# Graph attention and a top-2 expert layer on one core: two of four column groups of P in full precision

## The chip, the cores and the metric

The kernel runs on one core of a Trainium2 chip. A core has five engines with queues of their own: PE (TensorE, matrix products), DVE (VectorE), ACT (ScalarE), POOL (GpSimd) and SP (SyncE, here only DMA issues). They run side by side and wait for one another by semaphores. The metric is device time in microseconds (us) of one execution; less is better.

## The reference

```python
def gnn(x, adj, W, a):                       # x is layer-normalised, 4096 x 256
    Wh = x @ W
    e = leaky_relu((Wh @ a[:256])[:, None] + (Wh @ a[256:])[None, :], 0.2)
    e = where((adj > 0) | eye, e, -9e15)     # 4096 x 4096
    return softmax(e, axis=1) @ Wh
x = x + gnn(layernorm(x), adj, W, a)
# then a mixture of 8 experts: router, softmax, the best 2, and for each
# token the weighted sum of W2 @ gelu(W1 @ xe + b1) + b2 of its 2 experts
x = x + ffn(layernorm(x), Wr, br, ln_g, ln_b, W1, b1, W2, b2)
```

The inputs and outputs are float32, and the adjacency matrix has 4096 x 4096 entries.

## The kernel before, in words

Each engine has its own program, written out by hand; the order inside a program is the order in the code, and semaphores tie the programs together. There are three stages.

**Projection** (to about 69 us). x comes in as 32 tiles of 128 rows, is normalised, transposed and multiplied by W. Each tile of Wh stays in SBUF as the right operand of the attention product. Tiles 0 to 23 are kept as two float16 tensors, a high part (`wh[:, n, 0]`, written by ACT in L872) and a rest (`wh[:, n, 1]`, by DVE in L1070). Tiles 24 to 31 are kept in float32 in `wh32`.

**Attention** (about 69 to 690 us). A step i handles 128 rows of the 4096 x 4096 scores. DVE computes the scores of two steps ahead in two halves (`scores`, L1099) and masks those of the next step and takes their minimum (`masked`, L1107); ACT turns the adjacency rows into a bias (L854) and takes the exponentials (L884). The result P, 128 x 4096, is needed transposed. PE transposes it in G = 4 column groups of 8 blocks (`p_transpose`, L707) through two PSUM buffers `tp`; ACT copies a group out, scaled (`p_hi`, L892). Of groups 0 to GS - 1 that copy is float16, `pt_hi`, and DVE computes the rest of the rounding as a second float16 tensor (`p_lo`, L1112, into `pt_lo`). PE then multiplies (`av`): for a float16 group three products a block, high by high, high by rest and rest by high (L723 to L725), 24 in all; for a float32 group one product a block (L727), 8 in all. GS was 3: groups 0, 1 and 2 are float16 and group 3 is float32.

In the same loop earlier rows go on their way: step i - 1 is divided by its sum and added to x (L1118, L1122, L1130), its statistics are taken (L1136, L1143), POOL computes the scales (`row_scales`, L534 to L543) and DVE normalises it (`normalise1`, L1152). Step i - 2 has its router logits computed (PE L741, DVE L1160, L1166, L1171), its top two kept (`keep_top`, L1174 and L1179), turned into one-hots (L1183, L1184, L1188), and its position in the lists of the experts counted by PE (`router_pos`, L746 and L747). Step i - 3 gets its destination rows (`positions` to `keep_rows`, L1192 to L1203), and POOL scatters it to DRAM (L567). POOL also splits the weights of the experts into two float16 parts, one chunk a step (`split_w`, L525 and L528), and clears the diagonal of the mask (`diagonal`, L505).

The order of PE in a step is transposes 0 and 1, av of group 3 of the step before, the router's transposes (L733), av 0, logits (L741), transpose 2, av 1, transpose 3, av 2, router_pos. That of POOL is `cast_w` (L516), gates (L550 to L559), scatter (L567 twice), split_w, diagonal, row_scales. The code of DVE for a step has these lines in the part that the change touches:

```python
                if router:
                    experts(i - 2)
                if now:
                    p_lo(i, 2)
                if router:
                    keep_top(i - 2, u)
                if within(i, 0, T - 3):
                    scores(i + 2, u, 0)
```

**Experts** (about 690 us to the end). The scattered rows come back expert by expert, and PE multiplies them by the two float16 parts of W1 and W2 (L804 to L806, L820, L823). The change touches nothing of this stage.

Of the kernel before, what the change touches and what calls it, by code (L numbers as in the profile page):

```python
# [7 lines left out]
F32 = mybir.dt.float32  # L8
# [5 lines left out]
P = 128  # L14
# [8 lines left out]
def build(nc, x, adj, gnn_w, gnn_a, w_r, b_r, ln_g, ln_b, w1, b1, w2, b2, out):  # L23
# [16 lines left out]
    N, D = x.shape  # L40
    E = w_r.shape[1]
    HID = w1.shape[2]
    T = N // P
    KD = D // P
    HC = HID // P
    G = 4
    GJ = T // G
    GW = GJ * P
# [5 lines left out]
    RING = 4  # L54
    CHUNKS = 4
    CW = KD * HID // 2
    GS = G - 1
    TS = GS * GJ
    XC = 8
    TC = T // XC  # L60
# [15 lines left out]
    with ExitStack() as ctx:  # L76
        def sb(name, shape, dt, stack=ctx):
            return stack.enter_context(nc.sbuf_tensor(name, shape, dt))

        def sem(name):  # L80
            return ctx.enter_context(nc.semaphore(name))
# [25 lines left out]
        front = ExitStack()  # L107
# [3 lines left out]
        t2_row = sb("t2_row", [P, N], F32, front)  # L111
        sc = [sb(f"sc{u}", [P, N], F32, front) for u in range(2)]
        wh = sb("wh", [P, TS, 2, D], F16, front)
        wh32 = sb("wh32", [P, GJ, D], F32, front)
        pt_hi = [sb(f"pt_hi{g}", [P, GW], F16, front) for g in range(GS)]
        pt_lo = [sb(f"pt_lo{g}", [P, GW], F16, front) for g in range(GS)]
        pt32 = sb("pt32", [P, GW], F32, front)
        x_late = sb("x_late", [P, N], F32, front)
        wsp = [sb(f"wsp{u}", [P, 2 * CW], F16, front) for u in range(2)]
        xn = [sb(f"xn{u}", [P, D], F32, front) for u in range(2)]  # L120
# [112 lines left out]
        s_hi = sem("p_hi_done")  # L233
        s_lo = sem("p_lo_done")
# [87 lines left out]
        def within(i, first, last):  # L322

            return not isinstance(i, int) or first <= i <= last
# [142 lines left out]
        def _(pool):  # L467
# [50 lines left out]
            def split_w(e, q):  # L518

                i = CHUNKS * e + q  # L520
                u = q % 2
                pool.wait_ge(s_lo, GS * i + 2)
                pool.wait_ge(s_wf[u], 16 * (2 * e + q // 2 + 1))
# [132 lines left out]
        def _(pe):  # L656
# [41 lines left out]
            def p_transpose(i, u, g):  # L698
                if g % 2 == 0:
                    pe.wait_ge(s_e[g // 2], i + 1)  # L700
                if g == 1:
                    if within(i, 1, T):
                        pe.wait_ge(s_hi, G * i)
                elif g > 1 or within(i, 1, T):
                    pe.wait_ge(s_lo, GS * i + max(g - 1, 0))
                for c in range(GJ):
                    m = pe.transpose(tp[g % 2][:, c * P:(c + 1) * P], sc[u][:, (GJ * g + c) * P:(GJ * g + c + 1) * P], ident[:, :])  # L707
                m.then_inc(s_t, 1)

            def av(i, u, g):  # L710

                o = acc[u][:, 0:D]
                if g < GS:
                    pe.wait_ge(s_lo, GS * i + g + 1)
                else:
                    pe.wait_ge(s_hi, G * i + G)
                if g == 0 and within(i, 2, T):
                    pe.wait_ge(s_x1, X1 * (i - 2) + 3)
                for c in range(GJ):
                    j = GJ * g + c  # L720
                    cols = slice(c * P, (c + 1) * P)
                    if g < GS:
                        pe.matmul(o, pt_hi[g][:, cols], wh[:, j, 0, :], start=(j == 0), stop=False)  # L723
                        pe.matmul(o, pt_hi[g][:, cols], wh[:, j, 1, :], start=False, stop=False)  # L724
                        m = pe.matmul(o, pt_lo[g][:, cols], wh[:, j, 0, :], start=False, stop=False)  # L725
                    else:
                        m = pe.matmul(o, pt32[:, cols], wh32[:, c, :], start=False, stop=(c == GJ - 1))  # L727
                m.then_inc(s_av, 1)

            def router_t(i, r):  # L730
# [116 lines left out]
        def _(act):  # L847
# [39 lines left out]
            def p_hi(i, g):  # L887
                act.wait_ge(s_t, G * i + g + 1)
                if within(i, 1, T):
                    act.wait_ge(s_av, G * i + g - 3)  # L890
                dst = pt_hi[g] if g < GS else pt32
                act.activation(dst[:, :], tp[g % 2][:, :], ACT.Copy, scale=PSCALE).then_inc(s_hi, 1)  # L892

            def gate_exp(n, u):
# [108 lines left out]
        def _(dve):  # L1003
# [106 lines left out]
            def p_lo(i, g):  # L1110
                dve.wait_ge(s_hi, G * i + g + 1)
                dve.scalar_tensor_tensor(out=pt_lo[g][:, :], in0=tp[g % 2][:, :], scalar=PSCALE, in1=pt_hi[g][:, :],  # L1112
                                         op0=ALU.mult, op1=ALU.subtract).then_inc(s_lo, 1)


            def row_sum(n, u):
                dve.wait_ge(s_e[1], n + 1)
                dve.tensor_scalar(rinv[:, 0:1], rsum[u][:, 0:1], rsum[u][:, 1:2], PSCALE, ALU.add, ALU.mult).then_inc(s_x1, 1)  # L1118

            def row_reciprocal(n):  # L1120
                dve.wait_ge(s_x1, X1 * n + 1)
                dve.reciprocal(rinv[:, 1:2], rinv[:, 0:1]).then_inc(s_x1, 1)  # L1122
# [67 lines left out]
            def positions(n):  # L1190
                dve.wait_ge(s_pos, n + 1)
                dve.tensor_tensor(posb[:, :], rt_ps[:, 16:16 + E], count[:, :], ALU.add).then_inc(s_next, 1)  # L1192
# [13 lines left out]
            def attend(i, r, o):  # L1206

                u = r % 2
                v = 1 - u
                now, ahead = within(i, 0, T - 1), within(i, 0, T - 2)  # L1210
                behind, router, ranks = within(i, 1, T), within(i, 2, T + 1), within(i, 3, T + 2)
                back = (r + RING - 1) % RING
                back_o = o if r > 0 else o - 1
                if ranks:
                    positions(i - 3)
                if behind:
                    row_sum(i - 1, v)
                if ranks:
                    choose_rows(i - 3)
                if behind:  # L1220
                    row_reciprocal(i - 1)
                if ranks:
                    keep_rows(i - 3, (r + 1) % RING)
                if now:
                    p_lo(i, 0)
                    p_lo(i, 1)
                if ahead:
                    masked(i + 1, v)
                if behind:
                    add_attention(i - 1, v, back, back_o)  # L1230
                if router:
                    logits(i - 2, u)
                if behind:
                    stats1(i - 1, back)
                if router:
                    largest(i - 2)
                if behind:
                    moments1(i - 1)
                if router:
                    experts(i - 2)  # L1240
                if now:
                    p_lo(i, 2)
                if router:
                    keep_top(i - 2, u)
                if within(i, 0, T - 3):
                    scores(i + 2, u, 0)
                if router:
                    one_hots(i - 2, u)
                if behind:
                    normalise1(i - 1, v, back, back_o)  # L1250
                if router:
                    both_hots(i - 2)
                if within(i, 0, T - 3):
                    scores(i + 2, u, 1)
# [6 lines left out]
            for i in range(2 * RING):  # L1261
                attend(i, i % RING, i // RING)
# [151 lines left out]
```

## Time and profile before

| what | value |
|---|---|
| median of 3 runs | 1116.82 us (1110.28 to 1117.27) |
| the profiled execution | 1116.05 us, span of the trace 1114.5 us |
| PE busy | 983.5 us, 88% |
| DVE busy | 822.2 us, 74% |
| POOL busy | 814.8 us, 73% |
| ACT busy | 579.3 us, 52% |
| mean granted TensorE clock | 0.957 of full speed |

The span goes from the first to the last instruction; the profiled execution took 1.55 us more than that. The shares are of the span and mix three stages with different limits. A mean duration of a group counts each instruction from its own start to its own end, and neighbouring matrix products overlap, so that the distance between two starts can be much smaller than the duration.

### The profile page before, as it was taken

What the parts mean: (1) busy time and instruction counts of PE and PEld (TensorE: products, weight loads), DVE (VectorE), ACT (ScalarE), POOL (GpSimd) and SP (SyncE); (2) the same over time, 40 slices, a digit from 0 to 9 for tenths busy, and PEclk for the clock granted to TensorE, in tenths of its full rate; (3) what the DMA queues carried; (4) which work ended last, traced back from release to release, by engine and by line L of the source; (5) the groups of instructions that cost most, each with busy time, mean ns of one, the idle gap of its engine ahead of it and who ended that gap; (6) DMA issues with size and microseconds to landing.
All of it is one profiled execution on the core that took longest, in us unless ns stands there. A gap on an engine that the chain in (4) does not pass through costs nothing. (4 is left out here: it accounts for less than half of the span.)

```text
span 1114.5 us, 25515 instructions
## 1 busy us (share of the span) xinstructions
PE 983.5 (88%) x7566; PEld 822.3 (74%) x7567; DVE 822.2 (74%) x1563; ACT 579.3 (52%) x906; POOL 814.8 (73%) x910
## 2 busy tenths in 40 slices
PE   5959988899898888898988992799999999999995
PEld 4847877788787778787877882677777777777763
DVE  6859878888888888888887865457676666757663
ACT  3667676666675766676665740343433333343341
POOL 2218777888797888797878864278888888878763
PEclk9979999999999999999999996899999999999998
DMA  8164748575658485667566627774233232322231
GB/s 246 14 210 156 270 153 264 183 248 174 229 176 269 155 264 168 228 187 252 172 220 205 195 92 254 241 235 119 44 52 51 44 57 39 56 43 49 39 45 19
DMA packets 92201, 170.46 MB, mean 153 GB/s; under 512 B 19952, under 2 KB 69360, under 8 KB 83824
## 3 DMA queue, kind: packets, MB, share of 16 engines
q1 hardware_dynamic: 57296, 133.00, 34.5%
q0 software_dynamic: 24048, 26.23, 14.3%
q10 hardware_dynamic: 10800, 10.52, 3.1%
q8 instruction: 30, 0.49, 0.2%
q14 instruction: 27, 0.22, 0.1%
HBM read 136.91 MB, written 41.19 MB: 160 GB/s over the span
## 5 line engine op out<-in xcount | busy, mean ns | idle before, releaser
L723 PE MATMUL acc<-wh,pt_hi 128*128 128x256 f16 x768 | 211.2, 275 | 2.8 <-DVE pt_lo L1112 2.8
L971 ACT ACTIVATE hf<-tp,b_cols 128x256 f32<-128x256 f32 (+1 forms) x312 | 116.1, 459 | 187.4 <-PE tp L806 183.3
L724 PE MATMUL acc<-wh,pt_hi 128*128 128x256 f16 x768 | 211.2, 275 | 0.0
L725 PE MATMUL acc<-wh,pt_lo 128*128 128x256 f16 x768 | 211.1, 275 | 0.0
L567 POOL DMA_INDIRECT rows_dram<-rows,slot x64 | 161.3, 2520 | 38.6 <-POOL rows L559 26.4
L639 POOL DMA_INDIRECT out<-y_sb,yidx x71 | 118.9, 1674 | 92.2 <-issue 42.8
L820 PE MATMUL acc<-w_sb,h_hi 128*128 x568 | 170.9, 379 | 5.1 <-issue 3.8
L892 ACT ACTIVATE pt_hi<-tp 128x1024 f16<-128x1024 f32 x96 | 96.2, 1022 | 144.8 <-PE tp L707 144.4
L804 PE MATMUL tp<-x_hi,w_sb 128*128 128x256 f16 (+1 forms) x624 | 162.2, 265 | 2.6 <-DVE x_lo L1345 2.5
L806 PE MATMUL tp<-x_down,w_sb 128*128 128x256 f16 (+1 forms) x624 | 162.3, 265 | 0.0
L805 PE MATMUL tp<-x_lo,w_sb 128*128 128x256 f16 (+1 forms) x624 | 161.9, 265 | 0.0
L707 PE MATMUL tp<-ident,sc 128*128 128x128 f32 x1024 | 143.8, 294 | 14.2 <-ACT sc L884 12.4
L1099 DVE SCALAR_TENSOR_TENSOR sc<-t_row,s_col 128x2048 f32<-128x2048 f32 x64 | 151.6, 2372 | 0.1
L854 ACT ACTIVATE bias_sb<-adj_sb,big 128x2048 bf16<-128x2048 f32 x64 | 127.5, 2001 | 42.0 <-DMA adj_sb<-in_adj 41.7
L614 POOL TENSOR_SCALAR dz<-xs,dump 128x1 f32<-128x1 f32 x71 | 143.5, 2716 | 5.0 <-DMA xs<-rows_dram 3.9
L1107 DVE CUSTOM_DVE_ANT_0 sc<-sc,bias_sb 128x4096 f32<-128x4096 f32 x32 | 141.3, 4416 | 0.2 <-DVE sc L1099 0.2
L707 PEld LDWEIGHTS tp<-ident,sc 128*128 128x128 f32 x1024 | 126.4, 153 | 16.5 <-issue 14.7
L1112 DVE SCALAR_TENSOR_TENSOR pt_lo<-tp,pt_hi 128x1024 f16<-128x1024 f32 x96 | 115.5, 1221 | 25.6 <-ACT pt_hi L892 25.1
L884 ACT ACTIVATE sc<-sc,mn 128x2048 f32<-128x2048 f32 x64 | 127.6, 1994 | 2.8 <-DVE mn L1107 2.8
L1342 DVE CAST x_hi<-xg 128x512 f16<-128x512 f32 (+1 forms) x39 | 22.8, 584 | 138.9 <-ACT xg L960 127.1
L727 PE MATMUL acc<-wh,pt 128*128 128x256 f32 x512 | 122.7, 395 | 0.0
L823 PE MATMUL acc<-w_sb,h_lo 128*128 x568 | 113.0, 273 | 0.0
(170 smaller groups left out, 1953.9 us busy)
## 6 DMA issues: line engine op xcount, KB each, us to landing
adj_sb<-in_adj SPq DMA_DIRECT2D x64, 1024.0 KB
x_late<-in_L_ffn_W SPq DMA_DIRECT2D x32, 512.0 KB
wsplit_dram<-wsp SPq DMA_DIRECT2D x32, 512.0 KB, 2.9
w_sb<-wsplit_dram SPq DMA_DIRECT2D x32, 512.0 KB, 5.6
xs<-rows_dram ACTq DMA_DIRECT2D x32, 260.0 KB, 3.5
wsp<-in_L_ffn_W POOLq DMA_DIRECT2D x32, 256.0 KB
x<-in_x SPq DMA_DIRECT2D x32, 128.0 KB, 2.5
out<-x SPq DMA_DIRECT2D x32, 128.0 KB, 2.3
```

What stands on the lines that cost most here:

```text
L567: pool.indirect_dma_start(out=rows_dram[:, :], out_offset=bass.IndirectOffsetOnAxis(ap=slot[r][:, k:k + 1], axis=0), in_=rows[r][:, :], in ...
L614: pool.tensor_scalar(dz[:, s:s + 1], xs[r][:, s, D + 3:D + 4], 0.0, dump[:, s:s + 1], ALU.is_equal, ALU.mult).then_inc(s_dz, 1)
L707: m = pe.transpose(tp[g % 2][:, c * P:(c + 1) * P], sc[u][:, (GJ * g + c) * P:(GJ * g + c + 1) * P], ident[:, :])
L723: pe.matmul(o, pt_hi[g][:, cols], wh[:, j, 0, :], start=(j == 0), stop=False)
L724: pe.matmul(o, pt_hi[g][:, cols], wh[:, j, 1, :], start=False, stop=False)
L725: m = pe.matmul(o, pt_lo[g][:, cols], wh[:, j, 0, :], start=False, stop=False)
L804: pe.matmul(o, w_hi, x_hi[:, cols], start=(k == 0), stop=False)
L805: pe.matmul(o, w_hi, x_lo[:, cols], start=False, stop=False)
L806: m = pe.matmul(o, w_lo, x_down[:, cols], start=False, stop=(k == KD - 1))
L820: pe.matmul(acc[s][:, :], h_hi[u][:, (c * ns + s) * P:(c * ns + s + 1) * P], w_both, start=(c == 0), stop=False, skip_group_check=True)
L1099: dve.scalar_tensor_tensor(out=sc[u][:, cols], in0=t_row[:, cols], scalar=s_col8[:, bass.ds(n, 1)], in1=t2_row[:, cols], op0=ALU.add, op1= ...
L1107: dve.tensor_tensor_reduce(sc[u][:, :], sc[u][:, :], bias_sb[u][:, :], 1.0, 3.0e38, ALU.add, ALU.min, mn[u][:, 0:1]).then_inc(s_b, 1)
```

## The change

GS becomes G // 2 = 2, so that groups 0 and 1 of P stay float16 pairs and groups 2 and 3 are float32. Tiles 16 to 23 of Wh move from the float16 pair to `wh32`, and `pt32` becomes two buffers. Group 2 needs no `p_lo`, and DVE's call in the middle of the step goes. The waits in front of the transposes follow: a transpose that overwrites a `tp` buffer waits for whichever reads it last, ACT's copy where the group is float32 and DVE's `p_lo` where it is float16.

```diff
-    GS = G - 1
+    GS = G // 2
@@
-        wh32 = sb("wh32", [P, GJ, D], F32, front)
+        wh32 = sb("wh32", [P, T - TS, D], F32, front)
@@
-        pt32 = sb("pt32", [P, GW], F32, front)
+        pt32 = [sb(f"pt32{g}", [P, GW], F32, front) for g in range(GS, G)]
@@ p_transpose
-                if g == 1:
-                    if within(i, 1, T):
-                        pe.wait_ge(s_hi, G * i)
-                elif g > 1 or within(i, 1, T):
-                    pe.wait_ge(s_lo, GS * i + max(g - 1, 0))
+                if g >= GS:
+                    pe.wait_ge(s_lo, GS * i + g - GS + 1)
+                elif within(i, 1, T):
+                    pe.wait_ge(s_hi, G * (i - 1) + GS + g + 1)
@@ av
-                    pe.wait_ge(s_hi, G * i + G)
+                    pe.wait_ge(s_hi, G * i + g + 1)
@@
-                        m = pe.matmul(o, pt32[:, cols], wh32[:, c, :], start=False, stop=(c == GJ - 1))
+                        m = pe.matmul(o, pt32[g - GS][:, cols], wh32[:, j - TS, :], start=False, stop=(j == T - 1))
@@ p_hi
-                dst = pt_hi[g] if g < GS else pt32
+                dst = pt_hi[g] if g < GS else pt32[g - GS]
@@ attend of DVE
-                if now:
-                    p_lo(i, 2)
```

On PE the end of a step of the attention loop (the last block of av 2, router_pos, and the first transposes of the next step) reads so before:

```order
L723 MATMUL acc<-wh,pt_hi 128x256
L724 MATMUL acc<-wh,pt_hi 128x256
L725 MATMUL acc<-wh,pt_lo 128x256
L746 MATMUL rt_ps<-oh,tri 128x8 [waits onehot_done]
L747 MATMUL rt_ps<-oh,ones 128x8
L337 REGISTER_ALU
L337 COMPARE_AND_BRANCH
L707 MATMUL tp<-ident,sc 128x128 [waits p_lo_done,exp_half_done0]
L707 MATMUL tp<-ident,sc 128x128 x7
L707 MATMUL tp<-ident,sc 128x128 [waits p_hi_done]
```

and the same place of the changed kernel, from transpose 3 on (its lines are numbered one lower from here on):

```order
L706 MATMUL tp<-ident,sc 128x128 [waits p_lo_done]
L706 MATMUL tp<-ident,sc 128x128 x7
L715 ISA
L726 MATMUL acc<-wh,pt 128x256 [waits p_hi_done]
L726 MATMUL acc<-wh,pt 128x256 x7
L745 MATMUL rt_ps<-oh,tri 128x8 [waits onehot_done]
L746 MATMUL rt_ps<-oh,ones 128x8
L337 REGISTER_ALU
L337 COMPARE_AND_BRANCH
L706 MATMUL tp<-ident,sc 128x128 [waits p_hi_done,exp_half_done0]
```

The 24 float16 products of av 2 became 8 float32 products, which wait for ACT's copy alone, and the first transpose of the next step waits for that copy in place of `p_lo`.

On DVE the middle of a step, from the statistics of step i - 1 to its normalisation, reads so before:

```order
L1143 BN_AGGR mv<-bs 128x2 [waits x1_step,ln_var_eps_step]
L1171 MAX_INDEX idx<-top,lg 128x8 [waits router_step]
L1112 SCALAR_TENSOR_TENSOR pt_lo<-tp,pt_hi 128x1024 [waits p_hi_done]
L1174 TENSOR_TENSOR gap_l<-top 128x1
L1179 CAST idxf<-idx 128x2 [waits row_tags_done,router_step]
L1099 SCALAR_TENSOR_TENSOR sc<-t_row,s_col 128x2048 [waits p_transposed]
L1183 TENSOR_SCALAR oh<-iota_e,idxf 128x8 [waits router_step]
L1184 TENSOR_SCALAR oh<-iota_e,idxf 128x8
L1152 TENSOR_SCALAR rows<-x_0,mv,rs 128x256 [waits rows_scattered0,ln1_rstd,ln1_stats]
```

and in the changed kernel:

```order
L1142 BN_AGGR mv<-bs 128x2 [waits x1_step,ln_var_eps_step]
L1170 MAX_INDEX idx<-top,lg 128x8 [waits router_step]
L1173 TENSOR_TENSOR gap_l<-top 128x1
L1178 CAST idxf<-idx 128x2 [waits row_tags_done,router_step]
L1098 SCALAR_TENSOR_TENSOR sc<-t_row,s_col 128x2048 [waits p_transposed]
L1182 TENSOR_SCALAR oh<-iota_e,idxf 128x8 [waits router_step]
L1183 TENSOR_SCALAR oh<-iota_e,idxf 128x8
L1151 TENSOR_SCALAR rows<-x_0,mv,rs 128x256 [waits rows_scattered0,ln1_rstd,ln1_stats]
```

The rounding rest of group 2 and its wait for ACT are gone, and everything behind it follows directly on the router's index search.

## Rows read from the trace of the kernel before

**Rows 1.** Waits from 70 to 640 us: waiter, releaser, total us, times, longest.

```profile
PE rt_ps L746 <- DVE oh L1188: 43.6, 24, 2.7
DVE rows L1152 <- POOL rs L540: 40.6, 25, 2.1
```

**Rows 2.** Timeline of PE, the step from 411 us: start, duration, what, idle before.

```profile
411.37 0.18 PE L746 MATMUL rt_ps<-oh,tri 128*128 128x8 bf16 x1 [1.36 <-DVE oh L1188]
...
413.36 3.62 PE L727 MATMUL acc<-wh,pt 128*128 128x256 f32 x16
416.82 0.38 PE L733 MATMUL xt_ps<-ident,rows 128*128 128x128 f32 x2
...
424.42 0.27 PE L723 MATMUL acc<-wh,pt_hi 128*128 128x256 f16 x1
424.53 0.27 PE L724 MATMUL acc<-wh,pt_hi 128*128 128x256 f16 x1
...
429.81 0.18 PE L746 MATMUL rt_ps<-oh,tri 128*128 128x8 bf16 x1 [2.61 <-DVE oh L1188]
```

**Rows 3.** Timeline of DVE in the same step.

```profile
416.44 4.42 DVE L1107 CUSTOM_DVE_ANT_0 sc<-sc,bias_sb 128x4096 f32<-128x4096 f32 x1
...
422.30 1.21 DVE L1112 SCALAR_TENSOR_TENSOR pt_lo<-tp,pt_hi 128x1024 f16<-128x1024 f32 x1
423.43 0.46 DVE L1174 TENSOR_TENSOR gap_l<-top 128x1 f32<-128x1 f32 x1
...
423.89 2.34 DVE L1099 SCALAR_TENSOR_TENSOR sc<-t_row,s_col 128x2048 f32<-128x2048 f32 x1
...
429.27 0.41 DVE L1152 TENSOR_SCALAR rows<-x,mv,rs 128x256 f32<-128x256 f32 x1 [1.99 <-POOL rs L540]
```

**Rows 4.** Timeline of POOL in the same step.

```profile
417.26 4.43 POOL L567 DMA_INDIRECT rows_dram<-rows,slot  x1 [0.30 <-issue]
421.71 2.15 POOL L525 TENSOR_TENSOR x_late<-x_late,wsp 128x1024 f32<-128x1024 f32 x1
424.07 3.06 POOL L528 TENSOR_SCALAR wsp<-x_late 128x1024 f16<-128x1024 f32 x1 [0.21 <-POOL x_late L525]
427.21 0.43 POOL L505 TENSOR_TENSOR bias_sb<-bias_sb,off_diag 128x128 bf16 x1
```

**Rows 5.** Single lines of the whole trace: durations in ns, least, median and most.

```profile
L525 POOL TENSOR_TENSOR x_late<-x_late,wsp x32: 2129/2141/6247, 86.4 to 659.4; 128x1024 f32<-128x1024 f32 x32
L528 POOL TENSOR_SCALAR wsp<-x_late x32: 1039/1040/3072, 92.9 to 661.7; 128x1024 f16<-128x1024 f32 x32
```

**Rows 6.** Windows of PE after three router_pos: length, PE busy, granted clock, DMA.

```profile
392.25:397.90 5.65, 5.65 (x28) 0.70 0.96 335
411.37:416.40 5.03, 5.03 (x33) 1.00 0.99 390
429.81:436.90 7.09, 7.09 (x34) 0.76 1.00 340
```

**Rows 7.** Timeline of PE: router_pos of other steps.

```profile
151.73 0.17 PE L746 MATMUL rt_ps<-oh,tri 128*128 128x8 bf16 x1
...
318.25 0.18 PE L746 MATMUL rt_ps<-oh,tri 128*128 128x8 bf16 x1 [0.44 <-DVE oh L1188]
...
392.25 0.18 PE L746 MATMUL rt_ps<-oh,tri 128*128 128x8 bf16 x1 [2.33 <-DVE oh L1188]
...
638.05 0.18 PE L746 MATMUL rt_ps<-oh,tri 128*128 128x8 bf16 x1 [1.56 <-DVE oh L1188]
```

**Rows 8.** Timeline of PE at the loop's first steps and its last.

```profile
109.34 0.28 PE L723 MATMUL acc<-wh,pt_hi 128*128 128x256 f16 x1 [2.11 <-DVE pt_lo L1112]
...
653.96 0.18 PE L746 MATMUL rt_ps<-oh,tri 128*128 128x8 bf16 x1 [0.19 <-DVE oh L1188]
...
669.51 0.17 PE L746 MATMUL rt_ps<-oh,tri 128*128 128x8 bf16 x1
```

**Rows 9.** Timeline of DVE in the projection.

```profile
48.76 0.16 DVE L1068 COPY sc<-tp 128x1 f32<-128x1 f32 x1 [0.42 <-ACT wh L872]
```

## The prediction

> **What bounds the kernel now.** The change touches the projection and the attention loop; only the attention loop has 32 steps to multiply a cost by. I read the list of waits of that loop first. Of 28 steps in its stretch PE stands still in 24 in front of router_pos, 1.8 us each on average, until DVE has written the one-hots; DVE stands still in 25 in front of the normalisation, 1.6 us each, until POOL has the scales [rows 1]. So PE waits for DVE and DVE for POOL, and neither is the pace setter in most steps.
>
> The timelines of one step tell what holds POOL. The step from 411.37 to 429.81 lasts 18.44 us on PE [rows 2]. POOL is never idle for more than 0.3 us from 417.26 to 427.64 [rows 4]: its second scatter takes 4.43 us and ends 0.9 us after DVE's masking (416.44 to 420.86) [rows 3, 4]; the weights' subtraction L525 follows at once; L528, which has a median of 1.04 us, takes 3.06 us, and DVE's L1099 (423.89 to 426.23) lies across its start [rows 3 to 5]. POOL's instructions are stretched by the DVE instruction beside them and end some 0.9 us after it. It goes the other way too: DVE's L1174, a subtraction of one column, takes 0.46 us and ends at 423.89, when POOL's L525 has just ended (423.86) [rows 3, 4]. The two exclude each other for these instructions, and the sum of both, one after the other, is the loop: scores (L1099), masking, the end of the scatter, L525, L528 with the other L1099, the diagonal, the scales, the normalisation. `p_lo` is not one of the excluding kind: L1112 ran from 422.30 to 423.51 inside L525 (421.71 to 423.86), and L525 took 2.15 us, its median being 2.14 [rows 3 to 5].
>
> The Trainium skill, "SBUF — State Buffer", section "SBUF: two separate sides", says that DVE and GpSimd hold a shared pair of ports one at a time, for a whole instruction, DVE where it has two SBUF inputs. `p_lo` has one input in PSUM, so by that rule too its removal frees nothing for POOL; were it held against POOL, its 1.2 us would leave the loop and the time would be that of the second rival below. By that rule, the trace agrees: L525 was 2.15 us under it.
>
> **The change part by part.**
>
> *PE, one group of 24 float16 products against 8 float32 ones.* The float32 group takes 416.82 - 413.36 = 3.46 us, start to next start. The float16 products start 424.53 - 424.42 = 0.11 us apart, 24 of them 2.62 us [rows 2]. Each step gains 0.84 us of PE work, 27 us over 32 steps. It lies directly in front of router_pos, in a place where PE waits. The cover is 1.36, 2.61 and 2.33 us in three neighbouring steps and 0.44 us in a poor one [rows 2, 7]. Four of the 28 steps have none (the one at 151.73 is such) [rows 1, 7]. Where the cover is gone, the price is what is missing of 0.84: at most 4 x 0.84 + 0.4 = 3.8 us. Behind a late router_pos, though, DVE has a 2.3 us score half before it needs PE again, and router_pos is not always late enough to matter. I take half, +1.9 us, ends 0 and 3.8.
>
> *The end of the loop.* In the last two steps DVE and POOL have no scores and no masking, and PE sets the pace: its waits are 0.19 us and none, with 15.55 us between 653.96 and 669.51 [rows 8]. Both steps pay: 0.84 - 0.19 + 0.84 = +1.5 us, and the last float32 group stands directly behind, so it goes to the end.
>
> *DVE, `p_lo` of group 2 gone.* It is 1.21 us [rows 3], 32 times 39 us, plus the waits for ACT in front of it. With it gone DVE comes to L1174 at 422.3 in place of 423.43 in the shown step. But there POOL's L525 runs until 423.86, and L1174 waits for that as it does now. L1099 then starts at 423.9 to 424.0, as now (423.89), and what comes behind is unchanged: L528 is stretched, the scales come at the same time, and DVE's wait in front of L1152 remains at its 1.99 us [rows 3, 4]. In steps in which L1174 comes after L525, L1099 starts up to 1.2 us earlier (the length of `p_lo`), and POOL is held up in L528 in place of the diagonal; the wait of DVE for the scales grows by the same. So the 39 us are worth 0 in the steady loop. The first two steps have no such scatter and are different: PE waits 2.11 us at 109.34 for exactly this `p_lo` [rows 8]. I take -2 us there, ends -3 and 0.
>
> *Waits moved.* The transpose of group 0 waits for ACT's copy of group 2 in place of DVE's rest of it, and av 2 for the copy. Group 2's `p_lo` ended at 423.51 and the transposes behind router_pos start after 429.81 [rows 2, 3], so neither wait is the last to end there: 0. ACT writes 128x1024 float32 in place of float16, as it does for group 3; I take 0.
>
> *Projection.* Tiles 16 to 23 lose DVE's L1070. DVE already waits 0.42 us for ACT in front of L1068 in a tile that has it [rows 9]. Worth 0. The buffers in SBUF are equally large (8 KB each way for Wh, 4 KB for P).
>
> *The granted clock.* This is the part that may bring something. After the wait of 2.33 us at 392.25 and of 2.61 us at 429.81 the granted clock was 0.70 and 0.76 of full speed, that is, partly at 1.2 in place of 2.4 GHz; after that of 1.36 us at 411.37 it was 1.00 [rows 2, 6, 7]. A slow step shows in the pace: PE needs 19.12 - 1.36 = 17.76 us from router_pos at 392.25 until it stands before the one at 411.37, and 18.44 - 2.61 = 15.83 us in the next step, and the steps last 19.12 and 18.44 us. Long waits and slow starts alternate. With 0.84 us more work the wait of 2.61 becomes 1.77 us, which lies between waits that were followed by full speed and by slow starts. If all 26 steps from 151.73 to 638.05, now (638.05 - 151.73)/26 = 18.70 us on average [rows 7], took 18.44, that would be -6.8 us. I take half, -3.4 us, ends -6.8 and 0.
>
> Sum: +1.9 + 1.5 - 2 - 3.4 = -2 us against the profiled execution's 1116.05 us, which is 0.8 us below the median of the runs shown: **1114 us**. A measurement of this kernel can tell about 1% (11 us) from no change.
>
> **The rivals.**
>
> *The clock stays full.* All terms as above, with -6.8 us for the clock and the late steps cured with it: 1116 - 6.8 - 2 + 1.5 = 1109 us. For it: the three windows [rows 6]. Against it: 1.77 us is untried. The skill has a rule for this: "TensorE: Matmul & The Clock Gate", section "HAM oscillation — how this bites in real kernels", says that a wait in each pass of a loop can bring the clock down anew each pass, and that giving TensorE work without such waits keeps it up. By that rule the added work is what cures the slow starts, and the time would be this rival's.
>
> *DVE was on the path after all.* If POOL and DVE don't exclude each other at L1174, L1099 starts 1.2 us earlier in each of some 30 steps and POOL is done with it earlier: -37 us, 1079 us. Against it: the ends at 423.86 and 423.89, and the 25 waits of DVE for POOL, which a shorter DVE only lengthens [rows 1, 3, 4].
>
> *PE becomes the bound (slower).* The place is router_pos. If the slow starts come in each step and the added group runs slow too, PE's 17.76 us become 17.76 + 0.84 + 0.56, the last because a slow-started float32 group would cost more than its 3.46 us (PE's slow steps are 1.93 us longer over some 7 us of work [rows 2, 6], about a quarter, and I put half of that on the group). That is 19.2 us against an average of 18.70: +0.5 us in 26 steps, 13 us, with the end +1.5: 1131 us. It decides as soon as the wait in front of router_pos is gone in most steps, that is, from PE work of 18.4 us on. If every step paid the full 0.84 us, it would be 1116 + 27 = 1143 us. Against it: 1.8 us of mean wait [rows 1], and that slow starts were seen after long waits, which would then be gone.
>
> **How the numbers follow.** The forecast (hidden on both sides, clock half cured): 0.58. The clock stays full, 1109: 0.19, of which a third goes beyond 1%. DVE on the path, 1079: 0.08. PE the bound, 1131 or more: 0.12, of which most is over 1% slower. Something else of either sign: 0.03. The bounds of the forecast's own terms give 1116 + (-3 - 6.8 + 1.5) = 1108 to 1116 + 3.8 + 1.5 = 1121. To leave no more than 2 in 10 outside, the range takes in the clock rival with 6 us to spare below and the beginning of the PE rival above: 1102 to 1130. Faster by over 1% (below 1105): 0.16; within 1%: 0.72; slower: 0.12.
>
> **What the changed profile would show.** Right: DVE's waits for POOL in front of the normalisation grow from 1.6 us to 2.2 or more; PE's waits in front of router_pos fall from 1.8 to about 1; L1099 starts right behind the end of L525; the steps take 18.4 to 18.8 us; the stretch from 653.96 on is 1 to 2 us longer. The clock rival: windows behind router_pos at 1.00 nearly all. The PE rival: no waits there, and steps over 19 us. The forecast is wrong if L1174 does not end with L525, or if the float32 products run at another price in their new place than 3.46 us a group.

## The result

Over 19 runs of each kernel the changed one takes 1118.34 us (1116.58 to 1121.96) and the one before 1114.68 us (1110.28 to 1117.27); the ratio is 1.0039, with a 95% interval of 1.0027 to 1.0051. So the change costs about 4.3 us by the ratio (the medians differ by 3.7 us). That is far inside the 1% that was called no change and inside the range, but the forecast was a small gain, and the measured loss is clear of noise: the sign was wrong. The forecast stood on the profiled execution's 1116.05 us, which is 1.4 us above the median of the 19 runs. The profiled execution of the changed kernel has a span of 1117.4 us, against 1114.5.

The list of waits of the changed kernel, from 70 to 640 us (waiter, releaser, total us, times, longest), answers to [rows 1]:

```profile
ACT bias_sb L853 <- DMA adj_sb<-in_adj: 59.1, 47, 5.3
DVE rows L1151 <- POOL rs L540: 54.4, 29, 3.0
PE rt_ps L740 <- ACT xnt L901: 31.9, 21, 3.6
PE rt_ps L745 <- DVE oh L1187: 9.0, 12, 1.7
```

Two lines go the way that was foretold: DVE waits longer for POOL (1.9 us a time in place of 1.6, where 2.2 or more was expected), and PE waits less in front of router_pos (L745; 0.75 us a time, where about 1 was expected). But PE's wait fell much further than by the 0.84 us a step that was added, from 43.6 to 9.0 us. The rest of it moved to another place, the router's logits (L740), where PE waits for ACT's copy L901, and ACT in turn waits for adjacency data. The same two lines of the kernel before, which the rows ahead of the prediction don't have:

```profile
ACT bias_sb L854 <- DMA adj_sb<-in_adj: 41.7, 37, 4.6
PE rt_ps L741 <- ACT xnt L902: 12.7, 11, 3.8
```

Why adjacency data comes later is told by POOL's line of [rows 5] in the changed kernel (least, median and most, ns):

```profile
L528 POOL TENSOR_SCALAR wsp<-x_late x32: 1039/3054/3149, 93.4 to 663.9; 128x1024 f16<-128x1024 f32 x32
```

The median of L528 was 1.04 us and is now 3.05 us. Of its 32 instructions 11 took over 2 us before, and 22 do now.

One step of the changed kernel in the timelines of DVE, POOL and SP shows the chain. It answers to [rows 3, 4]:

```profile
425.01 0.80 DVE L1173 TENSOR_TENSOR gap_l<-top 128x1 f32<-128x1 f32 x1
...
425.81 2.34 DVE L1098 SCALAR_TENSOR_TENSOR sc<-t_row,s_col 128x2048 f32<-128x2048 f32 x1
```

```profile
423.65 2.14 POOL L525 TENSOR_TENSOR x_late<-x_late,wsp 128x1024 f32<-128x1024 f32 x1
425.99 3.06 POOL L528 TENSOR_SCALAR wsp<-x_late 128x1024 f16<-128x1024 f32 x1 [0.21 <-POOL x_late L525]
```

```profile
429.21 0.35 SPq L371 DMA_DIRECT2D wsplit_dram<-wsp  x1
...
431.52 0.85 SPq L360 DMA_DIRECT2D adj_sb<-in_adj  x2
```

DVE's small L1173 ends when POOL's L525 does, and L1098 starts 0.2 us ahead of L528 and stretches it, as foretold. New is the third fence. SP has one queue, and its store of the split weights (L371) waits for L528; the next adjacency loads (L360) stand behind it in the queue. They are issued 18.2 us after router_pos of the step (413.31). In the step before the change in which L528 took 1.04 us, from 392.25 on, they went out at 408.63, that is after 16.4 us:

```profile
406.66 0.35 SPq L371 DMA_DIRECT2D wsplit_dram<-wsp  x1
...
408.63 0.85 SPq L360 DMA_DIRECT2D adj_sb<-in_adj  x2
```

What a late load does is to be seen in the step that follows. Before, behind the loads of 408.63, ACT did not wait for them:

```profile
414.59 4.12 ACT L854 ACTIVATE bias_sb<-adj_sb,big 128x2048 bf16<-128x2048 f32 x2
```

In the changed kernel, behind the loads of 431.52, first on ACT, then on PE:

```profile
436.63 2.00 ACT L853 ACTIVATE bias_sb<-adj_sb,big 128x2048 bf16<-128x2048 f32 x1 [1.54 <-DMA adj_sb<-in_adj]
440.25 2.00 ACT L853 ACTIVATE bias_sb<-adj_sb,big 128x2048 bf16<-128x2048 f32 x1 [1.62 <-DMA adj_sb<-in_adj]
442.15 0.36 ACT L901 ACTIVATE xnt<-xt_ps 128x256 f32<-128x256 f32 x1
```

```profile
442.57 1.03 PE L740 MATMUL rt_ps<-w_r_sb,xnt 128*128 128x8 f32 x4 [2.39 <-ACT xnt L901]
443.45 1.95 PE L706 MATMUL tp<-ident,sc 128*128 128x128 f32 x8
...
454.15 0.17 PE L745 MATMUL rt_ps<-oh,tri 128*128 128x8 bf16 x1
```

Both halves of the mask wait for their data, the copy for the router stands behind them, and PE waits 2.39 us in the middle of its step. After it the granted clock is low, as the windows of PE show (length, busy, granted clock, DMA):

```profile
431.70:442.00 10.30, 8.44 (x60) 1.00 0.93 316
442.00:454.00 12.00, 11.43 (x60) 0.72 0.63 225
```

The clock falls behind this wait, as it fell behind the two longer waits at router_pos in [rows 6]. The step lasts 22.41 us, from 431.74 to 454.15.

Where the 2.9 us of the two spans lie can be read from router_pos. Before, the 2nd came at 151.73 and the 28th at 638.05 [rows 7], and in the changed kernel:

```profile
154.01 0.17 PE L745 MATMUL rt_ps<-oh,tri 128*128 128x8 bf16 x1
...
639.55 0.18 PE L745 MATMUL rt_ps<-oh,tri 128*128 128x8 bf16 x1
...
686.05 0.19 PE L745 MATMUL rt_ps<-oh,tri 128*128 128x8 bf16 x1 [2.07 <-DVE oh L1187]
```

Up to the 2nd it is 2.3 us later; the 26 steps between take 485.5 us in place of 486.3; from the 28th to the last it takes 46.5 us, and 44.2 before (682.27 - 638.05). The expert stage behind took 0.8 us less. So in this pair of traces the loss lies at the two ends of the loop, and the steps between are 0.8 us faster. These are single executions; the experiments separate the parts over many runs.

### The profile page after: what moved, and what is told of

Same layout as the page of the kernel before. It is cut to its first block and busy times, and to the rows that moved or that the text cites. A ratio compares the mean times of both kernels' runs of the same rounds, so it can differ in the third digit from the quotient of the medians.

```text
span 1117.4 us, 24916 instructions
## 1 busy us (share of the span) xinstructions
PE 1002.8 (90%) x7310; PEld 834.4 (75%) x7311; DVE 803.4 (72%) x1523; ACT 579.2 (52%) x906; POOL 804.0 (72%) x910
## 5 line engine op out<-in xcount | busy, mean ns | idle before, releaser
L726 PE MATMUL acc<-wh,pt 128*128 128x256 f32 x1024 | 232.8, 381 | 1.5 <-ACT pt L891 1.5
L726 PEld LDWEIGHTS acc<-wh,pt 128*128 128x128 f32 x1024 | 190.9, 192 | 24.8 <-ACT pt L891 1.8
L567 POOL DMA_INDIRECT rows_dram<-rows,slot x64 | 143.7, 2245 | 39.5 <-POOL rows L559 26.4
L853 ACT ACTIVATE bias_sb<-adj_sb,big 128x2048 bf16<-128x2048 f32 x64 | 127.6, 2002 | 59.3 <-DMA adj_sb<-in_adj 59.1
L1098 DVE SCALAR_TENSOR_TENSOR sc<-t_row,s_col 128x2048 f32<-128x2048 f32 x64 | 155.3, 2430 | 2.3 <-PE tp L706 2.2
L706 PE MATMUL tp<-ident,sc 128*128 128x128 f32 x1024 | 135.7, 283 | 12.6 <-ACT sc L883 12.4
L722 PE MATMUL acc<-wh,pt_hi 128*128 128x256 f16 x512 | 144.7, 283 | 1.0 <-DVE pt_lo L1111 1.0
L723 PE MATMUL acc<-wh,pt_hi 128*128 128x256 f16 x512 | 144.2, 282 | 0.0
L724 PE MATMUL acc<-wh,pt_lo 128*128 128x256 f16 x512 | 144.0, 281 | 0.0
L614 POOL TENSOR_SCALAR dz<-xs,dump 128x1 f32<-128x1 f32 x71 | 130.9, 2371 | 5.6 <-DMA xs<-rows_dram 4.2
L706 PEld LDWEIGHTS tp<-ident,sc 128*128 128x128 f32 x1024 | 120.3, 149 | 14.2 <-issue 12.8
L1339 DVE CAST x_hi<-xg 128x512 f16<-128x512 f32 (+1 forms) x39 | 19.1, 490 | 141.2 <-ACT xg L959 134.4
L525 POOL TENSOR_TENSOR x_late<-x_late,wsp 128x1024 f32<-128x1024 f32 x32 | 103.5, 3235 | 11.2 <-DVE pt_lo L1111 10.5
```

What stands on the lines that cost most here:

```text
L567: pool.indirect_dma_start(out=rows_dram[:, :], out_offset=bass.IndirectOffsetOnAxis(ap=slot[r][:, k:k + 1], axis=0), in_=rows[r][:, :], in ...
L726: m = pe.matmul(o, pt32[g - GS][:, cols], wh32[:, j - TS, :], start=False, stop=(j == T - 1))
L1098: dve.scalar_tensor_tensor(out=sc[u][:, cols], in0=t_row[:, cols], scalar=s_col8[:, bass.ds(n, 1)], in1=t2_row[:, cols], op0=ALU.add, op1= ...
```

## The experiments

All times are medians, with the ratio to the kernel before on the same chip and its 95% interval; differences in us to the kernel before are worked out from the ratio. Lines of a list of waits are picked out of the whole list from 70 to 640 us. There are two theories. The first is the chain above: no rest on DVE, L528 stretched, SP's queue, adjacency loads, ACT's router copy, PE's logits. The second is that PE's added work alone costs what was measured, in late steps and at the end.

**1. Only PE's part.** The changed kernel, with DVE computing a rest that nobody uses (GL is 3; the rest goes over `pt_lo[0]`, which av 0 has read by then):

```diff
+                if now:
+                    p_lo(i, 2)
@@ p_lo
+                dst, hi = (pt_lo[g], pt_hi[g]) if g < GS else (pt_lo[0], pt32[0])
@@ split_w, and PE's waits on s_lo as before the change
-                pool.wait_ge(s_lo, GS * i + 2)
+                pool.wait_ge(s_lo, GL * i + 2)
```

> The changed kernel, but DVE still computes a rounding rest of group 2 where it did (into a buffer that is read by nobody at that time), so that DVE's order is that of before and PE's work that of the change. Before: 1114.7 us, the changed kernel 1118.3. Theory 1, late adjacency loads (without the rest, DVE's scores start ahead of POOL's L528 in nearly every step, L528 takes 3.05 us in place of 1.04, SP issues the next adjacency loads some 2 us later, ACT's mask and with it the router copy behind it come late, and PE stands in front of its logits): L528 is stretched in about half of the steps again, PE's waits at the logits fall from 32 towards 13 us, 1116 to 1117 us. Theory 2, PE's 0.84 us a step alone, paid in late steps and at the end of the loop: 1118 to 1120 us.

Measured: 1112.38 us, ratio 0.9975 (0.9956 to 0.9995). That is 2.8 us faster than before (the medians differ by 2.0 us), below either theory's span: the gain was in neither theory. The waits and L528:

```profile
ACT bias_sb L855 <- DMA adj_sb<-in_adj: 43.4, 35, 5.2
PE rt_ps L747 <- DVE oh L1190: 23.4, 17, 1.8
PE rt_ps L742 <- ACT xnt L903: 18.8, 14, 3.9
```

```profile
L529 POOL TENSOR_SCALAR wsp<-x_late x32: 1039/1046/3147, 91.9 to 657.1; 128x1024 f16<-128x1024 f32 x32
```

L528 is short again (13 of 32 over 2 us) and adjacency waits are as before. The added PE work does not cost time in sum here: it is the useful half of the change. Theory 2 falls.

**2. Only DVE's part.** The kernel before without its rest of group 2; PE's 24 products stay, with a rest of zero, which leaves out that part of the precision:

```diff
-                if now:
-                    p_lo(i, 2)
@@ at the start of DVE's program
+            dve.memset(pt_lo[2][:, :], 0.0)
@@ split_w, and PE's waits as in the changed kernel; GL is 2
-                pool.wait_ge(s_lo, GS * i + 2)
+                pool.wait_ge(s_lo, GL * i + 2)
```

> The kernel before without DVE's rest of group 2 and nothing else: group 2 keeps its 24 float16 products on PE, its rest is zero (that part of the result's precision is left out). Theory 1: the stretched L528 and the late adjacency loads appear without any PE work added; PE has 0.84 us a step more cover than in the change; L528 over 3 us in 20 or more steps, waits at the logits over 20 us, 1114 to 1117 us. Theory 2: DVE's part is neutral, L528 as before, 1113 to 1115 us.

Measured: 1122.66 us, ratio 1.0056 (1.0032 to 1.0079), 6.2 us slower by doing less (the medians differ by 8.2 us). This is more than theory 1 expected and far from theory 2.

```profile
ACT bias_sb L854 <- DMA adj_sb<-in_adj: 66.0, 42, 6.5
PE rt_ps L741 <- ACT xnt L902: 38.4, 20, 6.5
```

```profile
L529 POOL TENSOR_SCALAR wsp<-x_late x32: 1039/3057/3192, 92.7 to 674.1; 128x1024 f16<-128x1024 f32 x32
```

L528 took over 2 us in 21 of 32 steps. The two halves, 0.9975 and 1.0056, sum to +0.3%, beside the 0.39% of the change. Taking an instruction away from DVE is what makes the changed kernel slower.

**3 and 4. ACT's copy for the router between the halves of the mask,** in the changed kernel and in the one before:

```diff
                     mask(i + 2, u, 0)
-                    mask(i + 2, u, 1)
                 if within(i, 2, T + 1):
                     router(i - 2)
+                if ahead:
+                    mask(i + 2, u, 1)
```

> The changed kernel with ACT's copy for the router between the two halves of the mask, in place of behind both, so that PE's logits no longer wait for the second adjacency half. Theory 1: PE's wait at the logits falls from 32 us to under 8, steps over 20 us disappear, 1111 to 1115 us. Theory 2: the place of the copy hardly matters, 1117 to 1119 us.

> The kernel before with the same edit of ACT's order. Theory 1: the 13 us of waits at the logits go, late steps (20.5, 21.2 us) go, 1110 to 1114 us, a smaller gain than on the changed kernel. Theory 2: 1114 to 1115 us.

Measured: 1112.98 us, 0.9983 (0.9963 to 1.0003), and 1111.82 us, 0.9969 (0.9950 to 0.9988). The gain is larger on the changed kernel (from 1.0039 to 0.9983, against 1 to 0.9969), as theory 1 has it, though with these intervals the two gains are not clearly apart, and the interval of the first reaches above 1. In the changed kernel L528 is now stretched in 30 steps and the masks still wait 60.8 us, but this no longer reaches PE:

```profile
ACT bias_sb L853 <- DMA adj_sb<-in_adj: 60.8, 47, 5.2
...
PE rt_ps L740 <- ACT xnt L901: 1.7, 1, 1.7
```

So the late data cost mainly through the copy that stands behind the mask. That nothing else is lost by them is not shown by this.

**5 to 7. The adjacency loads one place earlier in SP's queue,** in the changed kernel, in the one before, and together with the edit of ACT:

```diff
-                    for h in range(2):
-                        if not (last and q == CHUNKS - 1):
-                            sp.wait_ge(s_mk[h], i + 1)
-                            load_adj(i + 1, h)
@@ here, in the first step alone, the same two loads of row 1 stay
                     if not (first and q < 2):
                         sp.wait_ge(s_wsp, i - 1)
                     load_w(e, q)
+                    for h in range(2):
+                        if not (last and q >= CHUNKS - 2):
+                            sp.wait_ge(s_mk[h], i + 2)
+                            load_adj(i + 2, h)
                     if q >= 1:
                         store_w(e, q - 1)
```

> The changed kernel with SP issuing the adjacency loads of a step one place earlier in its queue: before it waits for POOL's split of the weights (L528) to store it, in place of behind that wait. POOL, DVE, ACT and PE programs are untouched. Theory 1 (the stretched L528 acts through SP's queue on the adjacency loads): the masks' waits for adjacency data fall from 59 us to under 20, PE's waits at the logits from 32 to under 5, 1110 to 1114 us, though L528 is still stretched in 20 steps or more. If the stretched L528 acts in another way (POOL itself late): the time stays at 1117 to 1119 us.

> The kernel before with the same edit of SP's queue. Theory 1: masks' waits fall from 42 us to under 20, logits' waits from 12 to under 5, 1110 to 1113 us. Otherwise 1114 to 1115 us.

> The changed kernel with both the router copy between the mask halves on ACT and the adjacency loads one place earlier on SP. Theory 1: either alone takes PE's waits at the logits away, so the two together are within 2 us of the better one, 1110 to 1113 us; what is left is POOL's and DVE's loop of 18.4 us a step.

Measured: 1112.62 us, 0.9989 (0.9979 to 0.9998); 1110.41 us, 0.9963 (0.9949 to 0.9977); both edits on the changed kernel 1113.63 us, 0.9992 (0.9976 to 1.0008). The waits of the first of these:

```profile
PE rt_ps L749 <- DVE oh L1191: 37.9, 24, 3.1
...
ACT bias_sb L857 <- DMA adj_sb<-in_adj: 2.3, 2, 1.8
```

The masks' waits went from 59.1 to 2.3 us and PE's at the logits to nothing, while L528 is stretched in 30 of 32 steps. The queue of SP is the link, as theory 1 says, and the two edits take away the same thing and don't add up (experiment 7 came 0.6 us above its span). But the kernel before gained from it too, and stayed 2.2 us ahead of the changed one; the intervals, 0.9979 to 0.9998 and 0.9949 to 0.9977, do not overlap. So this chain does not explain the whole loss. The end of the loop, 46.5 against 44.2 us in these two traces as well, is as large as what is left. Experiment 8 takes the stretched L528 itself away.

**8. DVE held back.** The changed kernel, with one wait added and no work changed:

```diff
                 if within(i, 0, T - 3):
+                    dve.wait_ge(s_wsp, i + 1)
                     scores(i + 2, u, 0)
```

> The changed kernel with one more wait on DVE: the first half of the scores (L1098) starts only when POOL's L528 of the step is done, so that L528 can never be stretched by it. No work is added or taken away. Theory 1: L528 is 1.04 us in every step, the adjacency loads are issued 2 us earlier in most steps, PE's waits at the logits fall from 32 to about 10 us, 1111 to 1115 us: faster by a wait. If the stretching is harmless, DVE only starts later: 1118 to 1121 us.

Measured: 1110.06 us, ratio 0.9970 (0.9958 to 0.9983), 1 us better than expected. L528 is 1.04 us in each step, and these are the waits, and router_pos from the 2nd to the 28th step:

```profile
L528 POOL TENSOR_SCALAR wsp<-x_late x32: 1039/1040/1050, 92.4 to 654.8; 128x1024 f16<-128x1024 f32 x32
```

```profile
PE rt_ps L745 <- DVE oh L1187: 37.0, 26, 1.8
DVE rows L1151 <- POOL rs L540: 33.3, 29, 1.4
ACT bias_sb L853 <- DMA adj_sb<-in_adj: 25.1, 28, 2.8
```

```profile
152.66 0.17 PE L745 MATMUL rt_ps<-oh,tri 128*128 128x8 bf16 x1
...
630.46 0.18 PE L745 MATMUL rt_ps<-oh,tri 128*128 128x8 bf16 x1 [1.75 <-DVE oh L1187]
```

The 26 steps take 477.8 us in place of 485.5; one of them lasts 19.1 us, one 18.7, the first 16.9, and all others 18.3 to 18.5 us. The wait does not end the holding-up, it moves it: L534 (the first of the scales, one column) now takes 2.11 us in 28 of 32 steps beside DVE's L1098, and 0.19 us in every step of the changed kernel without the wait. SP's queue does not wait for L534; only the scales behind it do.

**9 to 11. The same wait in the kernel before, and with the early loads in both:**

```diff
                 if within(i, 0, T - 3):
+                    dve.wait_ge(s_wsp, i + 1)
                     scores(i + 2, u, 0)
@@ SP, experiments 10 and 11 alone: the whole edit of experiment 5
```

Experiment 9 is the kernel before with the wait, 10 the changed kernel with wait and loads, 11 the kernel before with wait and loads.

> The kernel before with the wait that held DVE's first score half until POOL's L528 was done. With the stretched L528 gone (11 steps have it) the adjacency loads come on time in most steps; PE keeps 0.84 us a step less work than in the changed kernel. If the added PE work is worth something through the granted clock (shorter waits at router_pos, fewer slow starts), this kernel is not faster than the changed one with the same wait in the steady part (477.8 us from the 2nd to the 28th router_pos), and about 2 us better at the end of the loop: 1109 to 1112 us. If the added work is only a cost, it is 2 to 5 us better than that one's 1110.1: 1105 to 1108 us.

> The changed kernel with DVE held and the adjacency loads one place earlier. The held kernel still had 25 us of masks' waits and a start 5 us later than the kernel with the early loads (152.7 against 147.3 us at the 2nd router_pos). If the two add up: 1104 to 1107 us; if the loads are no longer of use once L528 is short: 1109 to 1111 us.

> The kernel before with both edits. Against the changed kernel with both it shows what the change itself is worth once neither the stretched L528 nor late adjacency loads are in its way: 2 us faster at the end of the loop (44.2 against 46.5 us), and in the steady part equal if PE is hidden, 3 to 6 us slower if PE's long waits bring slow starts. 1103 to 1108 us.

Measured: 1111.84 us, 0.9960 (0.9942 to 0.9979); 1107.52 us, 0.9921 (0.9893 to 0.9950); 1111.31 us, 0.9948 (0.9931 to 0.9965). Experiment 9 is within its expectation, the one in which the added work is not only a cost. Experiment 10 is the fastest kernel of the study, and ahead of both kernels of the case; it came 0.5 us above its expected span. Experiments 10 and 11 differ by the change alone, on the same chip: there the change is worth 3.8 us by the medians (1107.52 against 1111.31), though the intervals of the two ratios overlap from 0.9931 to 0.9950. The executions themselves hardly overlap: 1106.74 to 1109.29 us in the 6 of experiment 10, 1109.16 to 1112.63 us in the 12 of experiment 11. Experiment 11 missed its span from above (1103 to 1108 us); its steady part is 2.6 us slower than that of experiment 10, a little under the 3 to 6 us of the case that PE's long waits cost clock. With the wait alone (experiments 8 and 9) the ratios are 0.9970 and 0.9960, which shows no difference between the two kernels. Their router_pos of the 2nd and the 28th step, of experiment 10 and of 11:

```profile
147.48 0.18 PE L749 MATMUL rt_ps<-oh,tri 128*128 128x8 bf16 x1 [1.79 <-DVE oh L1191]
...
627.94 0.18 PE L749 MATMUL rt_ps<-oh,tri 128*128 128x8 bf16 x1 [1.76 <-DVE oh L1191]
```

```profile
148.52 0.18 PE L750 MATMUL rt_ps<-oh,tri 128*128 128x8 bf16 x1 [2.61 <-DVE oh L1192]
...
631.60 0.18 PE L750 MATMUL rt_ps<-oh,tri 128*128 128x8 bf16 x1 [0.96 <-DVE oh L1192]
```

480.5 us with the change and 483.1 without it for the same 26 steps, and with the wait alone (experiments 8 and 9) 477.8 and 481.0 us (633.41 - 152.43). In both pairs PE has more work and the steps are shorter; each is a pair of single executions. The windows from 170 to 640 us of the changed kernel with DVE held and of the one before with DVE held give the granted clock:

```profile
170.00:640.00 470.00, 431.95 (x3071) 0.99 0.65 211
```

```profile
170.00:640.00 470.00, 421.02 (x3246) 0.96 0.65 211
```

In experiments 10 and 11 it is 0.98 and 0.96.

## Why the prediction was wrong

**What bounds the loop: right.** PE waits for DVE and DVE for POOL; where nothing else disturbs it, a step lasts 18.3 to 18.5 us in every kernel of the study, with either amount of PE work.

**PE's 0.84 us a step, +1.9 us for late steps: the work is hidden, as forecast; the 1.9 us do not show.** Experiment 1, which adds this work alone, is not slower, and its 26 steps take 481.9 us (633.45 - 151.53) in place of 486.3, so that no cost can be told from the gain. In the changed kernel the wait at router_pos was used up all the same, by the wait at the logits.

**The granted clock, -3.4 us: right in kind and sign.** Experiment 1 is 2.8 us faster than before, and the forecast's own terms for PE alone (+1.9, +1.5, -3.4) came to 0. Its granted clock from 170 to 640 us is 0.98, and 0.96 before. With DVE held the steps' granted clock is 0.99 with the added work and 0.96 without. The Trainium skill's rule in "TensorE: Matmul & The Clock Gate" ("HAM oscillation — how this bites in real kernels") says that waits in each pass of a loop can bring the clock down each time. In kind the traces agree: 0.72 in the 12 us behind a wait of 2.39 us, and 0.99 from 170 to 640 us in a loop whose waits at router_pos were 1.8 us at most. The full recovery that the rival drew from this rule did not come in the change as measured, since PE's waits moved to the logits: 0.97 from 170 to 640 us.

**DVE's `p_lo` gone, 0 in the steady loop: this is the step that failed.** The text said that where L1174 comes behind L525, "POOL is held up in L528 in place of the diagonal", and that this is worth 0. For POOL's own chain of work the sum is indeed the same: from the end of L525 to the end of L540 the median of the steps from 170 to 640 us is 5.23 us before and 5.21 in the changed kernel. But L528 has another customer: SP's queue waits for it, with the adjacency loads behind it, ACT's mask behind these, ACT's router copy behind that, and PE's logits last. The diagonal (L505) has none that soon. By itself the removal costs 6.2 us (experiment 2: ratio 1.0056). Of the effects of an instruction that ends 2 us later I had followed one engine, and not the queues that wait for the other result. Experiments 3, 5 and 8 cut the chain at three different links, and each takes the changed kernel from a ratio of 1.0039 to 0.9983, 0.9989 and 0.9970 (the interval of the first reaches 1.0003). Experiment 1 differs from the changed kernel by DVE's `p_lo`, with the waits that go with it: in the traces, its removal costs 2.5 us up to the 2nd router_pos, 3.6 us in the 26 steps and 1.1 us at the end.

**The start of the loop, -2 us: wrong in sign.** The changed kernel reaches the 2nd router_pos 2.3 us later. PE's wait of 2.11 us for `p_lo` at 109.34 [rows 8] became one of 1.54 us for ACT's copy at 109.86, and the first router_pos still comes at 130.7 us (130.5 before): DVE's earlier scores stretched POOL's L528 there too, 2.86 us at 107.47 (before it was L540, the scales themselves, 2.86 us at 109.26), and the scales came as late as before, at 112.27 us against 112.12. Between the first and the second, PE waits at the logits in both kernels, 3.75 us before and 3.63 now, and works at the low clock behind it; from there to router_pos it takes 11.4 us in place of 9.2, of which 0.84 are the added work and the rest a longer slow stretch (granted clock 0.72 in place of 0.82); why it is longer is not shown. With the early loads, which take this wait away, the 2nd router_pos comes at 147.3 us (experiment 5) and 147.5 (experiment 10), in place of 151.7 and 154.0.

**The end, +1.5 us: PE's part right, and a second part missed.** It is 46.5 against 44.2 us, +2.3, and the same 46.4 to 46.6 us came back in every kernel that has both parts of the change, 44.1 to 44.3 us in experiments 4, 6, 9 and 11. Experiments 1 and 2 both have 45.4 us: PE's work alone costs 1.2 us. Of the 2.3 us, 0.84 are in the last full step (16.39 against 15.55 us), and 1.4 in the one before, 17.29 against 15.91 us. There experiment 1, with PE's work alone, has 16.39 us, so that PE's work is 0.5 of the 1.4 us; the forecast had 0.65. The rest is again an order on POOL. Before:

```profile
637.52 0.45 POOL L543 TENSOR_SCALAR g<-va,rs 128x1 f32<-128x1 f32 x1 [0.22 <-POOL rs L540]
...
642.60 1.11 POOL L567 DMA_INDIRECT rows_dram<-rows,slot  x1 [0.95 <-POOL rows L559]
...
648.36 2.14 POOL L525 TENSOR_TENSOR x_late<-x_late,wsp 128x1024 f32<-128x1024 f32 x1
```

and in the changed kernel:

```profile
639.35 2.53 POOL L543 TENSOR_SCALAR g<-va,rs 128x1 f32<-128x1 f32 x1 [0.53 <-POOL rs L540]
...
645.24 4.74 POOL L567 DMA_INDIRECT rows_dram<-rows,slot  x1 [0.96 <-POOL rows L559]
...
651.27 2.15 POOL L525 TENSOR_TENSOR x_late<-x_late,wsp 128x1024 f32<-128x1024 f32 x1
```

POOL's L543, one column, is held beside DVE's L1098 (639.41 to 641.75) and lasts 2.1 us longer, so that the first scatter no longer starts ahead of DVE's masking (643.08 to 647.50 before, 644.58 to 648.99 now) and is held up too; L525 then starts 2.28 us behind the masking in place of 0.86, and PE waits 0.73 us for the one-hots at the step's end, where experiment 1 has no wait. The same 2.26 to 2.28 us stand in all six traces that have both parts of the change, and 0.84 to 0.86 us in the other seven. DVE's `p_lo` is in six of these seven; experiment 2, without it, has the L543 of 2.54 us but a scatter that starts 0.04 us ahead of the masking, and its step of 17.23 us has a lower granted clock (0.90). No experiment changed this place by itself.

**Rivals.** DVE was not on the path (the removal of its work costs). PE did not become the bound by its work; the sum of that rival has 0.56 us for the slow-started group, where half of a quarter of 3.46 us is 0.43. The clock rival's mechanism was at work in PE's part, and its time, 1109 us, was not reached by that part alone (1112.38 us in experiment 1).

**Open.** The loss of the changed kernel against the one before with the early loads in both (1112.62 and 1110.41 us): there PE no longer waits at the logits in either. The end of the loop, 2.3 us, is as much as these 2.2, but the steps between have the same 484.6 and 483.7 us although the clock should have helped; holding DVE, with the loads early, takes the changed kernel's ratio to the kernel before from 0.9989 to 0.9921, and that of the one before only from 0.9963 to 0.9948. So a stretched L528, or what else DVE's wait sets in order, costs a few us that don't go through SP's adjacency loads. POOL's own work is hardly later by it: from the end of L525 to the end of L540 the median is 5.22 us in experiments 5 and 6, with L528 stretched in 30 and 15 steps, and 5.13 us in experiments 10 and 11, with it short. Another way is in the list of waits: POOL's L516 waits until the store of the split weights has landed, which goes out when L528 is done. These waits are 33.8 us in experiment 5 and 3.1 in experiment 10, 24.2 in the changed kernel and 13.2 before. Whether they reach PE was not tried; the scatter behind L516 is in most steps held by DVE's masking anyway.

## What to carry to other kernels

Removing an instruction from an engine that waits anyway is not free of effects: what comes behind it starts earlier, and where two engines exclude each other, this decides whose instruction is held up. Ask of each instruction that may be held up who waits for its result, on all queues and the DMA queue too, and not only whether the engine's own sum stays the same. Where such an order is bad, one wait on the engine that has time (here a wait of DVE for POOL) can be worth more than the work saved: it took the changed kernel's ratio from 1.0039 to 0.9970, some 8 us of 1118.

## What the runs showed of the hardware

A small DVE instruction with two inputs in SBUF, L1173 on 128x1, took 0.80 us beside POOL's L525, and ended with it, while L1112 (1.2 us, one input in PSUM) ran inside L525 without stretching it. One input in SBUF was no protection: the cast L1178 of two columns took 2.80 us at 650.65 in the changed kernel, beside POOL's second scatter and L525, and 0.15 us at 425.74. POOL's L528 took 3.06 us beside DVE's L1098 and 1.04 us without. Small POOL instructions are held in the same way: L534 on 128x1 took 2.11 us beside L1098 and 0.19 us without, L543 2.53 and 0.45 us. A float32 group of 8 products of 128x256 takes PE 3.46 us and 24 float16 products of the same size 2.62 us. With DVE held, 26 steps were faster with the longer group (477.8 against 481.0 us), at a granted clock of 0.99 against 0.96 of full speed.
